# A decoder layer in one kernel: a fixed place for TensorE's heads loop in its instruction stream, the next group's x behind v, and most of v held until q and k have landed

## The reference

```
x = x + attn(layernorm(x))          # per token: 16 heads of 16; elu of q and k; head against head
x = x + cross_attn(layernorm(x), ctx_512)
x = x + experts(layernorm(x))       # 8 low-rank experts, the best two per token

# attn, for one token (H = 16 heads, HD = 16):
Q, K, V = xn @ Wq.T, xn @ Wk.T, xn @ Wv.T
Q1, Q2 = split(elu(Q)); K1, K2 = split(elu(K))
w1 = Q1 @ (K1.T @ V) * SCALE;  w2 = Q2 @ (K2.T @ V) * SCALE
attn = rms(rms(w1 - lmb * w2, g2) , g3) + ...   # then a gelu layer with W1, W2
```

## Time and profile before

| | |
|---|---|
| median of 3 runs | 696.79 us |
| these runs | 692.26 to 699.8 us |
| the profiled execution | 699.64 us |
| its span, first to last instruction | 697.9 us |
| mean granted TensorE clock | 0.951 of full |
| PE busy | 630.3 us (90%) |
| heads loop, first `head_scores(0)` of group 1 to that of group 7 | 79.14 to 224.14 us |

### The profile page before, as it was taken

One profiled execution on the slowest core, in us unless ns is written; L12 is line 12 of the kernel. 1 busy time (PEld: TensorE's weight loads), 2 busy tenths in 40 slices (PEclk: granted clock), 3 DMA queues, 4 the chain that ended last, 5 costly groups with the idle time before them and its releaser, 6 DMA issues.

```text
span 697.9 us, 21372 instructions
## 1 busy us (share of the span) xinstructions
PE 630.3 (90%) x8338; PEld 588.0 (84%) x8338; DVE 467.8 (67%) x1138; ACT 385.8 (55%) x852; POOL 358.5 (51%) x401
## 2 busy tenths in 40 slices
PE   4686989789977877879999999999999999999997
PEld 3565768677867877779999999999999999999997
DVE  3844636848655554797878768668777777776772
ACT  3443446557755465756757756756545564555432
POOL 0021245966784777577654653553464446543322
PEclk9787999979988799999999999999999999999999
DMA  8748666446538435321120220110111011100000
GB/s 284 70 73 101 110 103 104 107 71 113 103 64 159 133 122 174 114 69 54 46 70 32 84 84 16 54 39 16 39 39 40 1 38 38 38 0 16 16 16 31
DMA packets 84152, 50.27 MB, mean 72 GB/s; under 512 B 31321, under 2 KB 83809, under 8 KB 84065
## 3 DMA queue, kind: packets, MB, share of 16 engines
q1 hardware_dynamic: 84064, 49.07, 31.0%
HBM read 23.88 MB, written 12.58 MB: 52 GB/s over the span
## 4 chain that ended last, share of the span: by engine, by line
PE 69%; DVE 9%; issue 7%; ACT 5%; SPq 4%; DMA 4%; POOL 2%; POOLq 0%; DVEq 0%; ACTq 0%
PE banks L687 54%; PE banks L806 4%; PE banks L740 3%; PE banks L824 3%; SPq L567 2%; PE banks L842 1%; ACT L1223 1%; DMA h_qk<-p_qk 1%; SPq L552 1%; PE banks L755 1%; DVE m_hT_lo L1584 1%; POOL f_hT_lo L1989 1%; ACT m_hT_hi L1229 1%; DMA c_x<-x_scratch 1%; DMA n_v<-in_L_attn_Wv_dram 1%
## 5 line engine op out<-in xcount | busy, mean ns | idle before, releaser
L1989 POOL TENSOR_TENSOR f_hT_lo<-f_hs,f_hT_hi 128x512 fp32r<-128x512 f32 x64 | 86.9, 1358 | 112.5 <-ACT f_hT_hi L1336 112.5
L2005 POOL TENSOR_TENSOR h_rh<-h_ms,mhalf 128x16 f32<-128x16 f32 x32 | 94.6, 2964 | 2.4 <-DVE h_wn L1788 1.9
L1755 DVE SCALAR_TENSOR_TENSOR f_hs<-banks,nbic,f_h 128x256 f32<-128x256 f32 x128 | 54.6, 479 | 47.1 <-PE banks L687 47.1
L687 PE MATMUL banks<-woT_hi,f_hT_lo 128*128 128x256 f32 x256 | 74.4, 291 | 0.3 <-POOL f_hT_lo L1989 0.3
L687 PE MATMUL banks<-f_adT_hi,lbT_lo 128*128 128x256 f32 x256 | 73.6, 287 | 0.6 <-DVE f_adT_lo L1743 0.6
L687 PE MATMUL banks<-f_adT_hi,lbT_hi 128*128 128x256 f32 x256 | 72.4, 283 | 0.0
L687 PE MATMUL banks<-f_adT_lo,lbT_hi 128*128 128x256 f32 x256 | 72.3, 283 | 0.0
L687 PE MATMUL banks<-f_xT_hi,wiT_lo 128*128 128x256 f32 x256 | 71.7, 280 | 0.0
L687 PE MATMUL banks<-f_xT_lo,wiT_hi 128*128 128x256 f32 x256 | 71.5, 279 | 0.0
L687 PE MATMUL banks<-f_xT_hi,wiT_hi 128*128 128x256 f32 x256 | 71.5, 279 | 0.0
L687 PE MATMUL banks<-woT_hi,f_hT_hi 128*128 128x256 f32 x256 | 71.1, 278 | 0.0
(11 more groups left out here) (265 smaller groups left out, 2018.1 us busy)
## 6 DMA issues: line engine op xcount, KB each, us to landing
h_qk<-p_qk SPq DMA_DIRECT2D x64, 128.0 KB, 4.5
xin<-in_x_dram SPq DMA_DIRECT2D x16, 256.0 KB, 4.9
h_v<-p_v SPq DMA_DIRECT2D x128, 32.0 KB
attn_scratch<-h_wn SPq DMA_DIRECT2D x16, 256.0 KB, 2.9
m_w<-attn_scratch SPq DMA_DIRECT2D x16, 256.0 KB, 3.7
m_x<-in_x_dram SPq DMA_DIRECT2D x16, 256.0 KB, 3.0
x_scratch<-m_y SPq DMA_DIRECT2D x16, 256.0 KB, 2.5
c_x<-x_scratch SPq DMA_DIRECT2D x16, 256.0 KB, 2.8
```

Source lines behind the costliest of these rows:

```text
L687: ins = pe.matmul(acc, left(a), right(b), start=first and n == 0, stop=last and n == 2, skip_group_check=skip)
L1755: ins = dve.scalar_tensor_tensor(out=f_hs[:, j % 2, c * T:(c + 1) * T], in0=bank[HB[j]][:, c * T:(c + 1) * T], scalar=nbic[:, f:f + 1], in ...
L1989: pool.tensor_tensor(lo, f_hs[:, j % 2], hi.bitcast(F32), ALU.subtract).then_inc(f_hlo, 1)
L2005: pool.tensor_tensor(h_rh[:, H * i:H * i + H], h_ms[:, H * i:H * i + H], mhalf[:, 0:H], ALU.pow).then_inc(h_rhd, 1)
```

## The change

Three edits. Before its heads loop, PE gets a directive (`addr_align`) by which the loader fills in empty instructions until the next one stands 33 instructions past a multiple of 128 in PE's stream (at most 127 of them). SP's list gets both halves of the next x behind the last v of a step. And SP waits, ahead of the last twelve of the sixteen v transfers of a group, until all eight q and k transfers of this group have landed.

```diff
+FETCH = 256
+HEADS_AT = 33
...
                     if c == 0:
                         sp.wait_ge(p_vcopy, nth(u, KD, b + 1))
                         apart(sp)
+                    if b == 0 and c == 1:
+                        for k in range(2):
+                            sp.wait_ge(h_qkin[u.slot][k], landed(u, ST))
+                            apart(sp)
                     for t in range(TG):
...
-            over_all(SU, [(7, store_w(1)), (3, tiles_in(0, 2)), (0, but_first_two(load_x(0))), (3, tiles_in(0, 3)), (3, values_in(0, 0)),
-                          (3, tiles_in(1, 0)), (3, tiles_in(1, 1)), (3, tiles_in(1, 2)), (3, tiles_in(1, 3)), (0, but_first_two(load_x(1))),
-                          (3, values_in(0, 1)), (3, values_in(1, 0)), (3, values_in(1, 1)), (2, tiles_in(0, 0)),
+            over_all(SU, [(7, store_w(1)), (3, tiles_in(0, 2)), (3, tiles_in(0, 3)), (3, values_in(0, 0)),
+                          (3, tiles_in(1, 0)), (3, tiles_in(1, 1)), (3, tiles_in(1, 2)), (3, tiles_in(1, 3)), 
+                          (3, values_in(0, 1)), (3, values_in(1, 0)), (3, values_in(1, 1)), (0, but_first_two(load_x(0))), (0, but_first_two(load_x(1))),
+                          (2, tiles_in(0, 0)),
...
+            pe.addr_align(FETCH // 2, HEADS_AT)
             over_all(SU, [(5, head_scores(1)),(3, project(1)), (3, project(2)), (4, head_scores(0)), (3, project_v(0)),
```

## The result

The changed kernel takes 709.48 us, median of 4 runs (706.15 to 711.82), beside 698.29 us of the kernel before on the same chip (4 runs, 692.26 to 699.8): a ratio of 1.0189, 95% interval 1.014 to 1.0238. It is slower, and the time lies above the forecast's range of 683 to 706 us. The profiled execution took 707.99 us with a span of 706.3 us.

The account below looks back on a forecast made before the run. PE with instruction-fetch stalls was taken to bound the heads loop (24.2 us a step), then a ring of SP, DMA, DVE and POOL (22.5). Group 7's v, 4.5 us earlier, gave 699.64 − 4.5 = 695.1 us; range 683 to 706.

Parts of the forecast that it names:

- DVE waits about 7 us a step for x: Sign of being right: in the heads loop, DVE's `p_moments` newly waits for xin's DMA, five times, about 7 us each.
- the two kinds of step: Heads loop before: two steps of 19.61 and 20.50 us, others 26.07 to 29.58; forecast to become steps all near 22.5 us.
- the end follows v of group 7: Last group's v loads: issued from 216.4 instead of 220.88 us, 4.5 us earlier, and that reaches the kernel's end.
- the stalls should then be few: PE in the heads loop: moved packet boundaries make the shortest stretch some 3.6 us, leaving few of 15.3 us of stalls.
- under 5 us: Sign of being right: PE's "issue" waits, those without a semaphore, total less than 5 us in the heads loop.
- The term that failed: SP's wait in each group: from first k issue to last q and k landing, 6.0 us, between 5.05 and 6.45.
- T(0) to T(7): Stretch from the issue of group 0's first k transfer to that of group 7: forecast from 50.5 to 210.4 us.
- the wrong ring: Heads loop: serial round of SP, DMA, DVE and POOL bounds each step, 6.0 + 8.3 + 4.7 + 2.7 + 0.8 = 22.5 us.
- SP's own list: SP's issues and wait in one heads-loop step: 6.0 + 8.3 + 1.2 + 7.5 = 23.0 us, without stores about 22.
- The place does nothing: Rival: PE keeps 24.2 us a heads-loop step, only the later v of group 7 counts, 701 us; chance 0.10.
- x is late, slower: Rival: heads-loop round at its upper end, 24.7 us, DVE waiting 9 us a step at the moments, 705 us; chance 0.19.
- up to 27 us: Fixed place in the heads loop: gain from 0 to 15.3 us of stalls plus low clock, 145.0 − 6 × 19.6.

Follow-up runs that it names:

- e1: The kernel before with only the fixed place 33 added: 690.91 us, ratio 0.9896 to the kernel before.
- e7: The kernel before with only the directive added, at place 84 instead of 33: 696.75 us, ratio 0.999 to the kernel before.
- e4: The changed kernel without the wait, so fixed place 33 and x behind v: 690.16 us, ratio 0.9885 to the kernel before.
- e8: The changed kernel with the wait ahead of the last four v transfers instead of the last twelve: 689.28 us, ratio 0.9891 to the kernel before.
- e2: The kernel before with only the x loads moved behind v: 696.98 us, ratio 0.9979 to the kernel before.
- e10: The changed kernel with the wait at the same place for one of two semaphores, the even tiles: 703.96 us, ratio 1.0069 to the kernel before.
- e5: The changed kernel with the x loads back in their old places: 708.39 us, ratio 1.015 to the kernel before.

## Why the prediction was wrong

**Right, and shown.** That PE's stalls stand at boundaries of 256-instruction packets, and that moving these is worth something: e1 and e7, one directive, two numbers, 5.8 us apart, the stalls where the count puts them. That PE isn't the bound in the changed kernel, and that SP's wait for its own transfers lies on the path that is: the chain. That DVE waits about 7 us a step for x, that PE then waits for `p_low` (4.8 us from 79 to 225 us), that the two kinds of step vanish: they did. And that the end follows v of group 7.

**Right in part: "the stalls should then be few".** In the changed kernel they are, 3.4 us. But with the same place and no standing of SP the waits without a semaphore are 7.7, 11.8 and 9.7 us in e1, e4 and e8, against 15.3 before, 16.1 in e2 and 12.3 in e7. So the sign "under 5 us" came true by more than the place. And the times don't go with these sums: e4 is as fast as e1. How much of the place's gain comes by way of these waits isn't shown.

**The term that failed: "a transfer lands 3.1 us after its issue at least, 4.5 in the median: 5.05 to 6.45, and I take 6.0, near the median, since four come in a row".** From the first k to the first of the twelve v it was 9.44, 7.82, 7.18, 7.44, 7.15, 7.53 and 7.33 us for groups 0 to 6, 7.7 on average: even the upper end, 6.45, was too low. Over seven steps that is 11.9 of the 13.5 us by which the stretch from T(0) to T(7) was longer than forecast (173.4 against 159.9); the twelve v took 8.3 us, as forecast, and the rest of the list was 1.9 us longer in all. Group 7 adds 1.5 us (7.5 instead of 6.0), and its v began at 231.99 us, not at 216.4. The wait ends with the last of the four, and I gave it the median of the earlier trace rows. That isn't the median of all 64 transfers, as the rows say: asked one by one, the trace of before has a landing for 16 of them, the first and the third of the runs of four of groups 0, 2, 4 and 6, never the last. (Of the 16 of x in the earlier trace rows it has 8.) In these four groups even the third k landed 9.3, 6.4, 6.5 and 6.1 us behind T, later than the 6.0 us taken for the last.

For the changed kernel the trace has every landing. Two of the four of the changed kernel's group 2, the first (issued at 102.92 us) and, with the one before it, the last (104.88 us):

```profile
DMA to landing us min/median/max: 3.5/3.5/3.5
```
```profile
DMA to landing us min/median/max: 4.8/5.0/5.1
```

The first lands 3.5 us behind its issue, the last 5.1 us. The DMA view of 102 to 111 us shows what moved meanwhile (GB/s in 40 slices of 0.23 us, then size and median landing):

```profile
GB/s 0 0 0 0 0 0 0 0 0 39 155 241 157 150 214 184 96 100 93 102 96 105 146 100 100 98 157 50 21 0 0 0 0 0 0 0 0 0 0 0
h_qk<-p_qk SPq DMA_DIRECT2D x4, 128.0 KB, 4.5
```

The rate is 150 to 241 GB/s at first, then around 100. 128 KB at 100 GB/s take 1.3 us, and SP issues one in 0.65 us. So the transfers line up: these four landed 1.2 us apart, the last 7.1 us behind T. Groups 4 and 5 are much the same. In the others the first took 4.1 to 6.0 us, and the last landed 7.2 to 7.7 us behind T all the same, in group 0 9.4. Why the rate falls to 100 GB/s no run tests.

e10 shows the same step from outside: waiting for the even tiles only, the last of which is third of the four, brought 5.5 us. In the changed kernel the last landed 0.3 to 1.3 us behind the third, 6.1 us in eight groups.

**The sum was made on the wrong ring.** I added up SP, DMA, DVE and POOL (22.5 us) and put SP's own list beside it as "about as long". Both carry the same landing, so both were short by the same 1.7 us a step; but e5 shows that the ring by way of DVE isn't the one that binds. Only at the first k of group 2 did SP wait for POOL, 2.2 us. SP's own waits of the kernel before would have given the sum in one line: 139.1 us of issuing in seven steps, plus seven times SP's standing for its own landings. With 3.4 us each, as I had it, 162.9 us, a little less than the 165.4 before; with the 4.6 us measured (32.0 / 7), 171.1, and with the 2.2 us for POOL 173.3, where 173.4 was measured. The sign of the loop's change hung on 1.2 us a group.

**The rivals.** "The place does nothing" falls by e1. "x is late, slower" gave the right sign and nearly the time (705 us), but by a mechanism that e2, e4 and e5 rule out: the slower side came from the wait, and I had it priced below what SP had to spare.

**The gain that wasn't forecast alone.** e1 makes plain that even without SP's standing the place is worth 7.5 us and not the up to 27 us of the earlier trace rows: the steps from group 3 on have other bounds of 22 to 26 us.

## What to carry to other kernels

Before a wait is added to a queue's program, add up what that queue waits for already: its issuing time plus the new wait against the length of the stretch tells whether the wait is hidden. Here a wait on its own transfers held up every issue behind it. If such a wait must be, put it behind issues that don't need it (e8: the same wait, no cost). A wait for a run of transfers lasts until the last has moved, so price it by the landing of the first and, for each one behind it, its size over the rate seen in the trace (here 3.5 + 3 × 1.2 us), not by the median landing of one; and look which transfers that median is made of. And where PE stalls without a semaphore inside long rows of short matmuls, count instructions between the stalls: if they are 256 apart, moving the loop by a few dozen instructions cost nothing that could be measured and gave 1% here. Of the two places tried, the one whose shortest packet lasts longer (3.6 us by the count, not 1.5) was the better; more than these two weren't tried.

## What was not expected of the hardware

Where the packet boundary falls is worth 5.8 us of this kernel between the places 33 and 84, with the same instructions on all engines but for 51 empty ones ahead of PE's loop. The stalls don't vanish at the better place: in e1 PE still stands 7.7 us in the loop, in e4 11.8 us. Four transfers of 128 KB issued 0.65 us apart landed about 1.2 us apart (group 2 of the changed kernel), at about 100 GB/s. DVE standing 34.2 us for a late x cost nothing, while SP standing 35.2 us cost 19 us against the same kernel without the wait (709.48 against 690.16).
